# Residuals preset in PSUM by ScalarE for all but two tiles, and the copies of the down weights in other places, in an attention and FP4 feed-forward kernel

## The chip, the cores and the metric

The kernel runs on one core of a Trainium2 chip. The metric is the device time of one execution in microseconds. The engines are TensorE (PE, with its weight loads as PEld), VectorE (DVE), ScalarE (ACT), GpSimd (POOL) and the queue that SyncE issues (SPq).

## The reference

The input `x` is 64 sequences of 128 rows of 256. What is computed, cut to what matters here:

```
x  = x + xattn(layernorm(x), ctx, ctx, Wq, bq, Wout, bout)   # correlation, top 12 shifts, weighted rolls
xn = layernorm(x)
gate = q(xn) @ q(w_gate).T ;  y = q(xn) @ q(w_up).T           # 256 -> 704
h = silu(gate) * y
out = x + q(h) @ q(w_down).T                                  # 704 -> 256
```

`q` is a blockwise quantization to FP4 and back: each block of 16 values is divided by its largest magnitude / 6, set on a grid of 8 magnitudes with a sign, and multiplied by that scale again. The last line holds what the change is about: the product with the down weights and the addition of `x`, the residual.

## The kernel before

The first part (to about 90 us of the span) loads `x` and the context, does the attention, quantizes the weights and turns most of them. The feed-forward part then goes over 64 tiles of 128 rows, in 32 pairs (NP = 32). Every engine has its own list of work, written out by hand, in stages of one pair; semaphores with constant counts tie the lists together. There is no planner.

In stage n **TensorE** (the loop at L1130) does `down` of tile 2n-7, `gate_and_up` of tiles 2n and 2n+1, and `down` of tile 2n-6. `gate_and_up` (L1108) fills three PSUM banks per tile: 18 products, six of 512 columns for each of two banks and six of 384 for the third. Behind the second bank ScalarE may start SiLU (`silu`, L711), behind the third VectorE may multiply (`gate_up`, L1375). `down` (L1066) is 17 products of 256 columns into one bank, 6 or 7 in turn for most tiles.

The residual can be added in two ways. For a **preset** tile, TensorE first opens the bank with one product of 256 columns (`open_down`, L1128, ahead of the third bank of a `gate_and_up`); it has to wait until the result of the tile two before, which stands in the same bank, has been read (`out_ready`, L293). ScalarE then overwrites the bank with the scaled tile of `x` (`preset_x`, L782), `down` accumulates onto it, and ScalarE writes the scaled sum to SBUF (`residual` of ScalarE, L716). For an **added** tile there is no opening and no presetting: `down` starts a new sum, and VectorE scales it and adds `x` in one instruction (`residual` of VectorE, L1457). Before, the added tiles are 1, 5, 9 ... 53, fourteen in all; tiles 0 to 61 without these are preset, 48 in all; the last two have an addition of their own on VectorE (L1451).

**ScalarE** in stage st (the loop of `for st in range(1, END)`) does, in this order: result of tile 2st-8 (L716), squares of a later pair (L753), the scales (L764), result of tile 2st-7, SiLU of tile 2st, preset of tile 2st-6, normalising of pair st+3 (L743), SiLU of tile 2st+1, preset of tile 2st-5, then the split of h of pair st-1 (`split_h`, three long instructions of 1408 columns, L650, L651, L653) and the split of x of pair st+2 (`split_x`, the same three lines with 512 columns).

**VectorE** in stage st does the two products of pair st-1 (L1375), their block maxima (L1492), the grid steps of pair st-2 (`offset_h`, which waits for ScalarE's split of h, L1172; `grid_h`, `high_h`) and of x, the added residual if there is one, the inverse scales (L1511), the products of x, and the scaling of h (L1486) and x (L1479). **GpSimd** does the low halves of h (L545) and adds the attention result to `x` (L599). **SyncE** issues the transposing transfers of h and x, the stores and the loads of the attention result, in order.

The **down weights** are turned on TensorE in five fills, numbers 8 to 12 (`transpose_weights`, L978), into banks 6 and 7, and copied to SBUF by ScalarE (`evacuate_weights`, L338 and L339). Fills 8 and 9 are turned ahead of the loop. Before, fill 10 is turned behind pair 0, fill 11 inside pair 2, fill 12 behind pair 2. ScalarE copies fill 8 ahead of its loop, fill 9 in stage 1 behind the first SiLU, fill 10 at the end of stage 1, fill 11 in stage 2 behind the first SiLU, fill 12 in stage 2 behind the second SiLU and ahead of the split of h. `filler` puts products without use on TensorE where it would have to wait.

Of the kernel before, what the change touches and what calls it, by code (L numbers as in the profile page):

```python
# [87 lines left out]
def build(nc, x, ctx, wq, bq, wout, bout, w_gate, w_up, w_down, out):  # L88
    es = ExitStack()
    with es:  # L90
# [182 lines left out]
        def tile_ok(i):  # L273
            return 0 <= i < B

        def added(i):
            return i % 4 == 1 and i // 2 < NP - 4

        def preset(i):
            return not added(i) and 0 <= i < 2 * NP - 2  # L280

        def n_added(i):
            return (min(i, 2 * (NP - 4) - 1) + 3) // 4

        def n_preset(i):
            return i + 1 - n_added(i)
# [355 lines left out]
        def _(act):  # L642
# [141 lines left out]
            def residuals(i):  # L784
                if tile_ok(i) and not added(i):
                    residual(i)
# [50 lines left out]
            for st in range(1, END):  # L837
                j, n = st - 1, st + 2
                if st < NP:
                    residuals(2 * st - 8)  # L840
                    square_x(st + 4)
                    scale_high(st)
                    residuals(2 * st - 7)
                    silu(2 * st)
                    preset_x(2 * st - 6)
                    if st <= 2:
                        evacuate_weights(act, range(GU_FILLS + 2 * st - 1, GU_FILLS + 2 * st))
                    normalise_x(st + 3)
                    if st == NP - 1:
                        split_h(j)  # L850
                        preset_x(2 * st - 5)
                    silu(2 * st + 1)
                    if st == 2:
                        evacuate_weights(act, range(GU_FILLS + 4, len(FILLS)))
                    if st < NP - 1:
                        preset_x(2 * st - 5)
                        split_h(j)
                    split_x(n)
                    if st == 1:
                        evacuate_weights(act, range(GU_FILLS + 2, GU_FILLS + 3))  # L860
                elif st == NP:
                    residual(2 * NP - 8)
                    preset_x(2 * NP - 6)
                    preset_x(2 * NP - 5)
                    last_split(0)
                    residual(2 * NP - 7)
                    preset_x(2 * NP - 4)
                    preset_x(2 * NP - 3)
                    residual(2 * NP - 6)
                    residual(2 * NP - 5)  # L870
                    last_split(1)
                    residual(2 * NP - 4)
                    keep_turned(0)
                    keep_turned(1)
                    residual(2 * NP - 3)
                    keep_turned(2)
                    keep_turned(4)
# [3 lines left out]
        def _(pe):  # L881
# [63 lines left out]
            def filler(n, k):  # L945
                for _ in range(n):
                    pe.matmul(bank(k)[:, 0:P], ones[:, :], ident[:, :], start=True, stop=True)  # L947
# [160 lines left out]
            def gate_and_up(i):  # L1108
                if i == 0:
                    pe.wait_ge(s["f_turned"], 16)  # L1110
                else:
                    pe.wait_ge(xT[(i // 2) % 2], 16 * (i // 4 + 1))
                need(pe, s["h_steps"], K_H * ((i - 2) // 2) + 1 + i % 2 if i >= 2 else 0)
                gu_bank(i, 0)
                gu_bank(i, 1).then_inc(s["gate_done"], 1)
                if i == 6:
                    pe.wait_ge(s["w_ev"], len(FILLS))
                if i >= 6:
                    open_down(i - 6)
                gu_bank(i, 2).then_inc(s["gu_done"], 1)  # L1120

            def open_down(j):
                if tile_ok(j) and preset(j):
                    if j // 2 == NP - 3:
                        pe.wait_ge(s["h_steps"], K_H * (NP - 1) + 1)
                    else:
                        out_ready(pe, j - (4 if j // 2 == NP - 2 else 2))
                    pe.matmul(bank(down_bank(j))[:, 0:D], ident16[:, :], dT_hi[:, 0, :], start=True, stop=False).then_inc(s["o_open"], 1)  # L1128

            for n in range(NP + 4):  # L1130
                if n == NP:
                    open_down(2 * NP - 6)
                    open_down(2 * NP - 5)
                if n == NP + 2:
                    out_ready(pe, 2 * NP - 5)
                    turn_last(0)
                if tile_ok(2 * n - 7):
                    down(2 * n - 7)
                if n == NP + 2:
                    turn_last(1)  # L1140
                if n == NP:
                    open_down(2 * NP - 4)
                if pair_ok(n):
                    if n == 2:
                        pe.wait_ge(s["w_ev"], GU_FILLS + 2)
                        filler(5, 7)
                    gate_and_up(2 * n)
                    if n == 2:
                        transpose_weights(GU_FILLS + 3)
                    gate_and_up(2 * n + 1)  # L1150
                if n == 0:
                    pe.wait_ge(s["w_ev"], GU_FILLS + 1)
                    filler(7, 6)
                    transpose_weights(GU_FILLS + 2)
                if n == 2:
                    pe.wait_ge(s["w_ev"], GU_FILLS + 3)
                    filler(12, 6)
                    transpose_weights(GU_FILLS + 4)
                if tile_ok(2 * n - 6):
                    down(2 * n - 6)  # L1160
                if n == NP:
                    open_down(2 * NP - 3)


        @block.vector
        def _(dve):
# [437 lines left out]
            for st in range(2, END):  # L1604
# [5 lines left out]
                if st < NP:  # L1610
                    if pair_ok(p):
                        offset_h(p)
                    scales(st)
                    if pair_ok(p):
                        grid_h(p)
                    if pair_ok(xa):
                        offset_x(xa)
                    if pair_ok(p) and st < NP - 1:
                        high_h(p)
                    if pair_ok(xa):  # L1620
                        grid_x(xa)
                    if tile_ok(2 * st - 7) and added(2 * st - 7):
                        residual(2 * st - 7)
                    inverses(st)
                    if pair_ok(xa):
                        products_x(xa)
                    if scaled(st):
                        dve.wait_ge(sc, 2 * (st - SC0) + 2)
                    if pair_ok(j):
                        scaling_h(j)  # L1630
                    if st == NP - 1:
                        high_h(p)
                        turned_product(p, 0, 1).then_inc(s["z_lo"], 1)
                    if pair_ok(xb):
                        scaling_x(xb)
                    largest_x(st + 3)
# [42 lines left out]
```

## Time and profile before

| | |
|---|---|
| time, median of 3 runs | 466.32 us (466.32 to 467.92) |
| the profiled execution: its time, its span | 466.81 us, 465.0 us |
| busy, share of the span: PE, DVE, ACT, POOL | 95%, 93%, 88%, 54% |
| chain that ended last: PE, ACT, DVE | 68%, 4%, 3% |
| L1128 opening products | x48 |
| L782 presets, L716 results on ACT | x48, x48 |
| L1457 added residuals on DVE | x14 |
| clock granted to TensorE, the 40 slices of the page | 9 (nine tenths or more) in each |

A share of busy time is a mean over the whole span; the attention part ahead of 90 us differs from the feed-forward part. In the rows further down, the first number of a line of the timeline is the start in the span, the second the length, and the square bracket gives how long the engine had been idle and who released it. An instruction of ScalarE or VectorE can start some 0.1 us ahead of the end of the one before it, so its price in a full list is the distance from start to start.

### The profile page before, as it was taken

Reading aid. Unit: us, or ns where it says so; the run is one execution under the profiler, and the core shown is the slowest. Engines: PE = TensorE matmul, PEld = TensorE weight load, DVE = VectorE, ACT = ScalarE, POOL = GpSimd, SP = SyncE. Lnnn points to the kernel's source line nnn. Section 1 sums busy time; section 2 is a strip of 40 time slices with the busy share of each in tenths; the row PEclk is TensorE's granted clock in tenths of the full one; section 3 lists DMA queues with packets and bytes.
Section 4 is the critical chain, followed back from the end, with each engine's and each line's share of the span. In section 5 each row is a group of like instructions: output and inputs, shape, how many; then the busy total and the mean of one; then the engine's idle time right before and its main releaser. Section 6 shows DMA issues by size and latency. Waiting matters only on the chain.

```text
span 465.0 us, 10105 instructions
## 1 busy us (share of the span) xinstructions
PE 443.0 (95%) x3436; PEld 298.7 (64%) x3436; DVE 431.3 (93%) x766; ACT 408.7 (88%) x710; POOL 252.7 (54%) x346
## 2 busy tenths in 40 slices
PE   4889998998989999999999999999999999999997
PEld 4778887755555666666666666666666666666676
DVE  3699979789899999999999999999999999999894
ACT  3369979889999999999999999999999999987684
POOL 4167772573555555666655566666666666433330
PEclk9999999999999999999999999999999999999999
DMA  7999911252446666665666766656656675656653
GB/s 241 339 348 350 357 43 35 69 137 46 90 93 141 140 141 130 149 132 131 131 132 130 137 138 143 141 130 143 142 132 134 139 143 111 128 111 132 122 122 94
DMA packets 162003, 67.95 MB, mean 146 GB/s; under 512 B 126368, under 2 KB 161696, under 8 KB 161952
## 3 DMA queue, kind: packets, MB, share of 16 engines
q1 hardware_dynamic: 161952, 67.31, 61.7%
q8 instruction: 27, 0.44, 0.4%
q14 instruction: 24, 0.20, 0.1%
HBM read 27.38 MB, written 9.18 MB: 79 GB/s over the span
## 4 chain that ended last, share of the span: by engine, by line
PE 68%; ACT 4%; DVE 3%; issue 2%; DVEq 0%; ACTq 0%
PE ps L1083 15%; PE ps L1061 14%; PE ps L1063 14%; PE ps L1062 14%; PE ps L1086 8%; PE ps L1128 2%; ACT h_c L653 1%; ACT h_c L650 1%; DVE y_h L1486 1%; PE ps L947 1%; DVE bm L1511 0%; ACT ps L782 0%; PE ps L1096 0%; ACT a_xT L716 0%; DVE ctx_sb L1380 0%
## 5 line engine op out<-in xcount | busy, mean ns | idle before, releaser
L1061 PE MATMUL ps<-guT_hi,a_xT 128*128 128x512 f16 (+1 forms) x384 | 138.7, 361 | 4.1 <-DVE hb L1375 3.0
L1063 PE MATMUL ps<-guT_hi,a_xT 128*128 128x512 f16 (+1 forms) x384 | 138.7, 361 | 0.0
L1062 PE MATMUL ps<-guT_lo,a_xT 128*128 128x512 f16 (+1 forms) x384 | 138.7, 361 | 0.0
L1083 PE MATMUL ps<-dT_hi,hqT 128*128 128x256 f16 x704 | 124.4, 273 | 0.4 <-ACT ps L782 0.3
L545 POOL TENSOR_TENSOR ctx_sb<-w_q_lo,sl 128x704 f16<-128x704 f16 x60 | 90.2, 1523 | 4.1 <-DVE ctx_sb L1443 4.1
L1086 PE MATMUL ps<-dT_lo,hqT 128*128 128x256 f16 x384 | 87.3, 273 | 0.0
L1083 PEld LDWEIGHTS ps<-dT_hi,hqT 128*128 128x128 f16 x704 | 68.9, 98 | 10.4 <-ACT ps L782 0.7
L599 POOL TENSOR_TENSOR xs<-xs,w_raw 128x512 f32<-128x512 f32 x30 | 38.4, 1279 | 64.2 <-DVE ctx_sb L1380 57.8
L561 POOL TENSOR_TENSOR sl<-bm,sh 128x240 f16<-128x240 f32 (+2 forms) x33 | 31.1, 941 | 74.9 <-DVE y_h L1486 72.0
L711 ACT ACTIVATE w_raw<-ps,inv_gu 128x704 f32<-128x704 f32 x64 | 53.8, 840 | 15.8 <-PE ps L1063 15.6
L1061 PEld LDWEIGHTS ps<-guT_hi,a_xT 128*128 128x128 f16 x384 | 37.6, 98 | 38.6 <-issue 2.7
L1063 PEld LDWEIGHTS ps<-guT_hi,a_xT 128*128 128x128 f16 x384 | 37.6, 98 | 38.5
L1062 PEld LDWEIGHTS ps<-guT_lo,a_xT 128*128 128x128 f16 x384 | 37.6, 98 | 32.0
L1375 DVE SCALAR_TENSOR_TENSOR hb<-ps,h_in,w_raw 128x704 f32<-128x704 f32 x64 | 57.6, 936 | 0.1
L650 ACT ACTIVATE h_c<-y_h 128x1408 bf16<-128x1408 bf16 (+3 forms) x39 | 47.8, 1225 | 8.7 <-DVE y_h L1190 4.5
L1492 DVE TENSOR_REDUCE bm<-hb 128x88 f32<-128x1408 f32 x31 | 50.2, 1620 | 1.1
L653 ACT ACTIVATE h_c<-h_c,root 128x1408 bf16<-128x1408 bf16 (+3 forms) x39 | 50.8, 1303 | 0.0
L1486 DVE TENSOR_TENSOR y_h<-hb,bm 128x1408 f32<-128x1408 f32 x31 | 50.0, 1612 | 0.1
L651 ACT ACTIVATE h_t<-y_h 128x1408 f16<-128x1408 bf16 (+3 forms) x39 | 47.2, 1211 | 0.0
L1086 PEld LDWEIGHTS ps<-dT_lo,hqT 128*128 128x128 f16 x384 | 37.6, 98 | 5.8
L743 ACT ACTIVATE w_q_hi<-xs,s_nmr,s_r 128x256 f32<-128x256 f32 x62 | 33.6, 593 | 0.7 <-POOL s_nmr L593 0.7
L1172 DVE TENSOR_TENSOR h_t<-h_c,h_t 128x1408 f16<-128x1408 bf16 (+3 forms) x39 | 30.8, 791 | 3.2 <-ACT h_c L653 3.1
(189 smaller groups left out, 813.2 us busy)
## 6 DMA issues: line engine op xcount, KB each, us to landing
xs<-in_x_dram SPq DMA_DIRECT2D x16, 512.0 KB, 8.7
ctx_sb<-in_ctx_dram SPq DMA_DIRECT2D x16, 512.0 KB, 8.3
out_dram<-a_xT SPq DMA_DIRECT2D x64, 128.0 KB, 2.1
w_raw<-a_scratch SPq DMA_DIRECT2D x60, 128.5 KB, 2.7
hqT<-ctx_sb SPq DMA_TRANSPOSE x62, 3.7
w_raw<-in_L_ffn_w_down_dram SPq DMA_DIRECT2D x1, 704.0 KB, 8.1
w_raw<-in_L_ffn_w_gate_dram SPq DMA_DIRECT2D x1, 640.0 KB, 5.1
w_raw<-in_L_ffn_w_up_dram SPq DMA_DIRECT2D x1, 640.0 KB, 6.4
```

The source lines that it names most:

```text
L545: pool.tensor_tensor(hq[:, j % 2, t, FF:2 * FF].rearrange("p (ih r) -> p ih r", ih=IH), h_g.bitcast(F16).rearrange("p (ih t r) -> p t ih r ...
L650: act.activation(c.bitcast(BF16), top, ACT.Square, scale=ANCHOR_SLOPE * unit).then_inc(done, 1)
L653: act.activation(c.bitcast(BF16), c.bitcast(BF16), ACT.Square, bias=root[:, 0:1]).then_inc(done, 1)
L711: act.activation(sil[:, i % 2, :], gu_out(i)[:, 0:FF], ACT.Silu, scale=inv_gu[:, 0:1]).then_inc(s["sil_done"], 1)
L1061: pe.matmul(dst, xt[:, c, :], guT[0][:, c, n0:n1], start=(c == 0), stop=False)
L1062: pe.matmul(dst, xt[:, c, :], guT[1][:, c, n0:n1], start=False, stop=False)
L1063: last = pe.matmul(dst, xt[:, KC + c, :], guT[0][:, c, n0:n1], start=False, stop=(c == KC - 1))
L1083: last = pe.matmul(dst, hqT[:, j % 4, c, :], dT_hi[:, c, :], start=(c == 0 and not preset(j)), stop=(c == DCH - 1))
L1086: pe.matmul(dst, hqT[:, j % 4, c, :], dT_lo[:, c, :], start=False, stop=False)
L1375: dve.scalar_tensor_tensor(out=h_v, in0=gu_out(i)[:, FF:2 * FF].rearrange(split, ih=IH), scalar=h_in[:, 0:1], in1=sil[:, i % 2, :].rearran ...
L1486: dve.tensor_tensor(y_h[:, :].rearrange(runs, ih=IH, il=2), hb[:, :].rearrange(runs, ih=IH, il=2), bm[:, 2, 0:RUN_H].unsqueeze(1).unsqueez ...
L1492: dve.tensor_reduce(bm[:, 0, 0:RUN_H], hb[:, :].rearrange("p (ih b il) -> p b ih il", ih=IH, il=2), AX.XY, ALU.max, apply_absolute_value=T ...
```

## The change

The added tiles are now 0 and 1 alone, so tiles 2 to 61 are preset: 60 in place of 48. VectorE's list looks at both tiles of its stage, so it does the residuals of tiles 0 and 1 one behind the other in stage 4. The opening products begin in `gate_and_up(8)`, and the one of tile 61 is issued behind `down(59)` in place of ahead of it. On ScalarE fill 9 is copied at the end of stage 1, fills 10 and 11 at the end of stage 2, fill 12 at the start of stage 3. On TensorE fills 10 and 11 are turned behind pair 2, fill 12 between the two tiles of pair 3, with other counts of useless products; the wait for all copies goes from the inside of `gate_and_up(6)` to the place ahead of `down(0)`.

```
@@ added, n_added
-            return i % 4 == 1 and i // 2 < NP - 4
+            return i in (0, 1)
-            return (min(i, 2 * (NP - 4) - 1) + 3) // 4
+            return min(i, 1) + 1
@@ ScalarE, for st in range(1, END)
                 if st < NP:
+                    if st == 3:
+                        evacuate_weights(act, range(GU_FILLS + 4, len(FILLS)))
                     residuals(2 * st - 8)
...
                     preset_x(2 * st - 6)
-                    if st <= 2:
-                        evacuate_weights(act, range(GU_FILLS + 2 * st - 1, GU_FILLS + 2 * st))
                     normalise_x(st + 3)
...
                     silu(2 * st + 1)
-                    if st == 2:
-                        evacuate_weights(act, range(GU_FILLS + 4, len(FILLS)))
...
                     split_x(n)
                     if st == 1:
-                        evacuate_weights(act, range(GU_FILLS + 2, GU_FILLS + 3))
+                        evacuate_weights(act, range(GU_FILLS + 1, GU_FILLS + 2))
+                    if st == 2:
+                        evacuate_weights(act, range(GU_FILLS + 2, GU_FILLS + 4))
@@ TensorE, gate_and_up
-                if i == 6:
-                    pe.wait_ge(s["w_ev"], len(FILLS))
-                if i >= 6:
+                if i >= 8:
                     open_down(i - 6)
@@ TensorE, for n in range(NP + 4)
                     if n == 2:
-                        pe.wait_ge(s["w_ev"], GU_FILLS + 2)
-                        filler(5, 7)
+                        filler(5, 6)
                     gate_and_up(2 * n)
-                    if n == 2:
-                        transpose_weights(GU_FILLS + 3)
+                    if n == 3:
+                        transpose_weights(GU_FILLS + 4)
                     gate_and_up(2 * n + 1)
                 if n == 0:
                     pe.wait_ge(s["w_ev"], GU_FILLS + 1)
                     filler(7, 6)
+                if n == 2:
+                    filler(10, 6)
                     transpose_weights(GU_FILLS + 2)
-                if n == 2:
-                    pe.wait_ge(s["w_ev"], GU_FILLS + 3)
-                    filler(12, 6)
-                    transpose_weights(GU_FILLS + 4)
+                    transpose_weights(GU_FILLS + 3)
+                if n == 3:
+                    pe.wait_ge(s["w_ev"], len(FILLS))
+                if n == NP + 1:
+                    open_down(2 * NP - 3)
                 if tile_ok(2 * n - 6):
                     down(2 * n - 6)
-                if n == NP:
-                    open_down(2 * NP - 3)
@@ VectorE, for st in range(2, END)
-                    if tile_ok(2 * st - 7) and added(2 * st - 7):
-                        residual(2 * st - 7)
+                    for i in (2 * st - 8, 2 * st - 7):
+                        if tile_ok(i) and added(i):
+                            residual(i)
```

## Rows read from the trace of the kernel before

**Rows 1.** Stretch, busy us of PE, PEld, DVE, ACT, POOL; clock, DMA share, GB/s.
```profile
233.00:284.00 51.00, 51.00 (x337) 32.45 (x335) 50.83 (x70) 49.02 (x80) 32.36 (x38) 1.00 0.65 137
```

**Rows 2.** Timeline of ScalarE, stages 14 and 15 (start, length, engine, line, work).
```profile
250.78 0.46 ACT L716 ACTIVATE a_xT<-ps,inv_out 128x256 f32<-128x256 f32 x1
...
253.14 0.47 ACT L782 ACTIVATE ps<-xs,out_fac 128x256 f32<-128x256 f32 x1
253.54 1.09 ACT L743 ACTIVATE w_q_hi<-xs,s_nmr,s_r 128x256 f32<-128x256 f32 x2
255.17 0.85 ACT L711 ACTIVATE w_raw<-ps,inv_gu 128x704 f32<-128x704 f32 x1 [0.54 <-PE ps L1063]
255.92 0.47 ACT L782 ACTIVATE ps<-xs,out_fac 128x256 f32<-128x256 f32 x1
256.40 1.38 ACT L650 ACTIVATE h_c<-y_h 128x1408 bf16<-128x1408 bf16 x1
...
261.96 0.46 ACT L716 ACTIVATE a_xT<-ps,inv_out 128x256 f32<-128x256 f32 x1
...
272.99 0.45 ACT L716 ACTIVATE a_xT<-ps,inv_out 128x256 f32<-128x256 f32 x1
```

**Rows 3.** Timeline of TensorE, the opening product of tile 22, stage 14.
```profile
251.28 0.28 PE L1128 MATMUL ps<-dT_hi,ident 128*128 128x256 f16 x1
```

**Rows 4.** Timeline of TensorE, first products of tiles 56, 58 and 60.
```profile
404.14 0.38 PE L1061 MATMUL ps<-guT_hi,a_xT 128*128 128x512 f16 x1
...
415.20 0.38 PE L1061 MATMUL ps<-guT_hi,a_xT 128*128 128x512 f16 x1
...
426.18 0.38 PE L1061 MATMUL ps<-guT_hi,a_xT 128*128 128x512 f16 x1
```

**Rows 5.** Timeline of VectorE, stages 2 to 4.
```profile
115.11 0.89 DVE L1172 TENSOR_TENSOR h_t<-h_c,h_t 128x1408 f16<-128x1408 bf16 x1 [0.55 <-ACT h_c L653]
...
120.05 1.61 DVE L1486 TENSOR_TENSOR y_h<-hb,bm 128x1408 f32<-128x1408 f32 x1
...
127.55 0.89 DVE L1172 TENSOR_TENSOR h_t<-h_c,h_t 128x1408 f16<-128x1408 bf16 x1 [1.32 <-ACT h_c L653]
...
135.22 1.79 DVE L1375 SCALAR_TENSOR_TENSOR hb<-ps,h_in,w_raw 128x704 f32<-128x704 f32 x2
...
141.85 0.47 DVE L1457 SCALAR_TENSOR_TENSOR a_xT<-ps,inv_out,xs 128x256 f32<-128x256 f32 x1
```

**Rows 6.** Timeline of ScalarE: copy of fill 9, and the split of h in stage 2.
```profile
108.46 1.01 ACT L339 ACTIVATE dT_hi<-ps 128x1024 f16<-128x1024 f16 x1
...
123.52 1.37 ACT L650 ACTIVATE h_c<-y_h 128x1408 bf16<-128x1408 bf16 x1
```

**Rows 7.** Timeline of TensorE, tile 8: its first product and the opening inside it.
```profile
136.30 0.38 PE L1061 MATMUL ps<-guT_hi,a_xT 128*128 128x512 f16 x1 [0.82 <-DVE hb L1375]
...
140.21 0.28 PE L1128 MATMUL ps<-dT_hi,ident 128*128 128x256 f16 x1 [1.16 <-ACT a_xT L716]
```

**Rows 8.** Timelines of TensorE, ScalarE and VectorE near the end.
```profile
450.98 0.28 PE L1128 MATMUL ps<-dT_hi,ident 128*128 128x256 f16 x1 [0.33 <-ACT a_xT L716]
451.10 0.27 PE L1083 MATMUL ps<-dT_hi,hqT 128*128 128x256 f16 x1
...
451.71 0.46 ACT L716 ACTIVATE a_xT<-ps,inv_out 128x256 f32<-128x256 f32 x1
453.53 0.27 ACT L722 ACTIVATE sh<-bm 128x88 bf16<-128x88 f32 x1
...
455.95 0.52 DVE L1172 TENSOR_TENSOR w_q_lo<-w_q_lo 128x704 f16<-128x704 bf16 x1 [0.64 <-ACT w_q_lo L730]
```

**Rows 9.** TensorE's first work (timeline); the last microsecond, columns of rows 1.
```profile
7.34 1.06 PE L900 MATMUL ps<-ident,xs 128*128 128x128 f32 x4
...
11.54 0.60 PE L890 MATMUL ps<-ident,ctx_sb 128*128 128x128 f32 x4
...
464.00:465.00 1.00, 0.00 (x0) 0.00 (x0) 0.00 (x0) 0.00 (x0) 0.00 (x0) 0.81 0.08 27
```

## The prediction

> **What bounds the kernel now.** I read the busy times by stretch first. In the middle TensorE and VectorE are both full (51.00 and 50.83 of 51 us) and ScalarE is busy 49.02 of 51 [rows 1], so the share of busy time doesn't name one bound; the question is which ring of waits closes last. For that I took ScalarE's timeline, stage by stage, from the result of one tile 2st-8 to the next: 250.78 to 261.96 to 272.99, so 11.18 and 11.03 us, 22.21 for two stages [rows 2]. Then TensorE's timeline where ScalarE has little left to do, near the end: a stage with two openings takes 11.06 us (404.14 to 415.20), one with a single opening 10.98 (415.20 to 426.18) [rows 4]. That is what TensorE alone needs.
>
> The reader is to see a ring between ScalarE and TensorE. ScalarE writes the result of tile 2st-8 at 250.78; the opening product needs its bank and starts at 251.28, 0.04 us behind the end of that instruction [rows 2, 3]. From there TensorE runs without a pause to the second bank of the next tile, and ScalarE's SiLU waits for that at 255.17, having been idle 0.54 us. Behind SiLU come the preset, the split of h and the split of x, and then the next result at 261.96 [rows 2]. The length of this ring is 4.39 (250.78 to 255.17) + 0.75 (SiLU, to 255.92) + the preset + 5.56 (256.40 to 261.96). The preset costs 0.40 from start to start where nothing is waited for (253.14 to 253.54) and 0.48 at 255.92, where the split also waits for VectorE's scaled h [rows 2]. So the ring without VectorE is 4.39 + 0.75 + 0.40 + 5.56 = 11.10 us.
>
> **The middle.** Removed: one addition on VectorE in every second stage, twelve net (fourteen less the two new early ones), 0.47 us each or about 0.40 from start to start; 4.8 us of VectorE's work in all. Added for each: a preset (0.40) and a result (about 0.36, 0.46 long less the usual overlap) on ScalarE and an opening of 0.11 us on TensorE. In the even stages the second result goes in ahead of the first SiLU. The ring doesn't pass there: it is covered by the 0.54 us that ScalarE waits ahead of the second SiLU [rows 2], and 0.18 of that is left; without this cover each such stage would cost up to 0.36. In the odd stages the second preset comes between SiLU and the split of h, on the ring. There it meets a wait: the odd stage now takes 11.03 without a preset in that place, so 0.32 of its time is waiting for VectorE, who will be early. The odd stage goes from 11.03 to 11.10, the even one from 11.18 to 11.10 as the wait for VectorE (0.08) goes. Two stages: 22.20 against 22.21. TensorE with two openings in each stage needs 11.06 and so stays just under the ring. The 22 stages from 5 to 27 give 0.0 (from -0.2 to +0.1). VectorE gets slack that nothing uses.
>
> What it could be from both sides: if the ring did not bind, TensorE's 11.06 would, 22 x 0.045 = 1.0 us faster; if ScalarE's 0.18 were not enough, by 0.1 in each of 12 double stages, 1.2 us slower. I take the ring as it adds up.
>
> The Trainium skill, "ScalarE: Activation LUTs", in the part on the steps of an ACTIVATE, says that ScalarE writes to PSUM faster than to SBUF. By that the preset (to PSUM) would cost less than the result's 0.36, the ring would fall under TensorE's 11.06, and the middle would give up to -1.0 us. The rows have it the other way round: 0.47 long into PSUM, 0.46 into SBUF [rows 2], so I keep 0.40.
>
> **The start.** VectorE waits for ScalarE's split of h twice, 0.55 us at 115.11 and 1.32 at 127.55 [rows 5]. The copies stood ahead of these splits: fill 9 at 108.46 (1.01 us), fills 11 and 12 ahead of the split at 123.52 [rows 6]. With fill 9 behind the split, the first wait goes. The second split can then start when the scaled h of pair 1 is there, at 120.05 + 1.61 - 0.55 = 121.1 [rows 5] in place of 123.52, 2.4 earlier, and so the second wait goes as well. What is late next: VectorE itself, whose stage 4 would start at 135.22 - 0.55 - 1.32 = 133.35 [rows 5]. Fills 10 to 12 now cost ScalarE about 2.1 us (three copies of 0.5 to 0.9) between the split of x in stage 2 and the SiLUs of stage 3; queued behind them are these SiLUs and the split of h of pair 2, and VectorE waits for that. By my walk it comes only some 0.1 us ahead of need, so this cover is thin, and anything beyond it is passed on 1 to 1. TensorE turns fill 12 between the tiles of pair 3 and must wait for the copy of fill 10 there, about 0.7 us, which nothing on the ring sees.
>
> Then the gain is taken back. Tile 0 is now added by VectorE, behind the grid steps of stage 4, where tile 1 was: at 141.85 - 1.87 = 139.98, done 0.47 later at 140.45 [rows 5]. The opening of tile 2 inside tile 8 must wait for it. Before, it waited for ScalarE and stood at 140.21 [rows 7]. So TensorE, though it starts tile 8 about 1.1 us earlier (the gap ahead of 136.30 closes [rows 7]), stands at the opening for some 2.7 us and goes on at 140.4, 0.2 us later than before. Everything in the ring hangs on this place. **+0.2**, from +0.1 to +0.6.
>
> **The last stages.** Stage 27 now ends without a preset ahead of its split of h; with it the ring takes 11.10 and TensorE, which before could go on at its own pace there, opens tile 50 about 0.14 later. Tile 53 gets an opening in a stage where TensorE is the bound: 0.08 (11.06 less 10.98) to 0.11 [rows 4]. **+0.24**, from 0 to +0.3.
>
> **The end.** The opening of tile 61 stood at 450.98 and had waited, 0.33 us by the profile and about 0.5 in distance [rows 8]. Now `down(59)` goes first and starts about 0.5 earlier; 17 products at 0.11 (450.98 to 451.10 is 0.12 [rows 8]) put the opening at 450.98 - 0.5 + 1.86 = 452.34. But ScalarE's preset of tile 61 waits for it, and behind it in ScalarE's list stand the results of 58 and 59 and the scales of the last tile's split, for which VectorE waits at 455.95 [rows 8]. The result of 58 stood 0.73 behind the opening (451.71); it comes to 453.07, and two instructions of 0.36 to 0.38 later the scales start at 453.81 against 453.53. TensorE's 0.5 is lost, as it then waits for the last tiles' grid. **+0.28**, from -0.5 (if TensorE's order is all that counts) to +0.3.
>
> **The sum.** 0.0 + 0.2 + 0.24 + 0.28 = 0.7 us onto the profiled execution: span 465.0 to 465.7, its time 466.81 to 467.5. That execution is 0.5 above the median of 466.32, so the median becomes 467.0. No change from the old time can be told within 0.5% (2.3 us), and this is 0.15%.
>
> **The rivals.**
> *The clock falls in the long stall (the slower side).* TensorE's clock rose only some time after it began: four transposes take 1.06 us at 7.34 and 0.60 at 11.54. It fell again in the last microsecond (0.81 on the mean of it), in which TensorE issued nothing [rows 9]. The pause of 1.16 us at tile 8 [rows 7] left it at full clock; the new one of some 2.7 us is more than twice as long. If it falls to 1.2 GHz there, it stays so for up to 4.2 us (7.34 to 11.54), and half of these is lost, 2.1 us, with no slack in the ring to take it up: 467.0 + 2.1 = 469.1. It decides if the longer pause at tile 8 is enough for the clock to fall as it did at the end. Against it: useless products still fill stage 2, and tile 8 has work right before and behind. The Trainium skill, "TensorE: Matmul & The Clock Gate", Part 1, says just this: an array that has been idle is put back to half its clock and gets it back only after sustained work. Chance 0.25.
>
> *The start keeps its gain.* If the addition of tile 0 doesn't hold the opening, ScalarE is the next that is late. It follows VectorE's scaled h, which comes 1.87 earlier [rows 5] less 0.40 for the second addition, 1.5: 467.0 - 0.2 - 1.5 = 465.3. Against it: the order in VectorE's list is fixed, and 140.45 already assumes that both its waits are gone. Chance 0.08.
>
> *TensorE alone sets the pace.* VectorE's full 50.83 of 51 [rows 1] speaks for VectorE as the bound of today, and 4.8 us of it go. But TensorE's 11.06 caps that: -1.0, and the late 0.14 of stage 27 goes too: 465.8. For it: the ring is only 0.04 longer. Chance 0.15; with the rival before it, 464.2 or a little less, 0.05 of further chance.
>
> *ScalarE is short of room in its stage*, in steady stages or by the copies of stage 3 (beyond the 0.1 of cover): 1 to 2.5 us slower, up to 469.5. Chance 0.07.
>
> **How the numbers follow.** The forecast of 467.0 has 0.40, and by its bounds 466.0 to 467.6 for itself. The range goes from 465.0 (just below the case in which the start keeps its gain) to 469.1 (the clock falls). Faster by over 0.5% (under 464.0) takes two rivals at once, or a gain that I don't see: 0.08. Slower by over 0.5% (above 468.65) is most of the clock's chance and a part of the last: 0.24. The rest, 0.68, is no difference that can be told.
>
> **What would show it.** Right: L782 and L716 x60 and L1457 x2; two stages in the middle at 22.2 us; ScalarE's stages of 11.10 each, no longer 11.18 and 11.03; VectorE with gaps of some 0.2 us per stage; no gaps of VectorE at its 1st and 2nd `offset_h`; a pause of 2 to 3 us ahead of the first opening, released by VectorE's L1457 at about 140.4; preset of tile 61 waiting for TensorE. Wrong: stages of 11.06 or less, an opening of tile 2 ahead of 140, ScalarE's second SiLU without a wait in even stages, or a granted clock below 1 about 140 us.

## The result, and the profile after

The changed kernel takes 469.0 us in the median (466.69 to 470.09, 22 runs), the kernel before 466.62 (466.29 to 469.32, 22 runs alternating with it). The ratio is 1.0037, 95% interval 1.0025 to 1.0049: 1.7 us slower, clear of zero and inside the 0.5% that I had called no difference, while the medians lie 2.4 us apart. The profiled execution took 469.47 us, its span 467.7.

The page of the changed kernel: its busy times, the clock by slices, and the chain that ended last (each entry a share of the span).

```profile
PE 445.0 (95%) x3444; PEld 300.2 (64%) x3444; DVE 430.8 (92%) x754; ACT 415.0 (89%) x734; POOL 251.3 (54%) x346
...
PEclk9999999999998999999999999999999999999999
...
PE 69%; DVE 6%; issue 1%; ACT 0%; DVEq 0%; ACTq 0%
```

ScalarE left the chain (4% before), VectorE came up from 3% to 6%. One clock slice reads 8. That slice is a mean over 11.7 us, so short stretches follow. Their columns are those of [rows 1]; the last but two is the clock as a share of full speed.

```profile
233.00:284.00 51.00, 51.00 (x338) 32.47 (x336) 50.83 (x69) 50.04 (x86) 31.91 (x37) 1.00 0.63 133
80.00:84.00 4.00, 3.66 (x9) 2.56 (x10) 1.57 (x3) 3.12 (x5) 3.02 (x2) 0.58 0.00 0
142.00:145.00 3.00, 3.00 (x10) 1.12 (x9) 3.00 (x6) 0.98 (x2) 0.46 (x1) 0.52 0.44 106
```

The reader is to see two stretches near half speed (1.2 GHz), at 81 and at 142; I call each a fall. The kernel before shows 1.00 in both stretches in its profile (the one at 80 stands further down):

```profile
142.00:145.00 3.00, 3.00 (x18) 1.54 (x17) 3.00 (x5) 2.45 (x6) 1.47 (x2) 1.00 0.03 6
```

The timeline of TensorE at tile 8, which answers to [rows 7]:

```profile
136.03 0.38 PE L1061 MATMUL ps<-guT_hi,a_xT 128*128 128x512 f16 x1
...
138.19 0.38 PE L1062 MATMUL ps<-guT_lo,a_xT 128*128 128x512 f16 x1
138.40 0.38 PE L1063 MATMUL ps<-guT_hi,a_xT 128*128 128x512 f16 x1
141.17 0.28 PE L1126 MATMUL ps<-dT_hi,ident 128*128 128x256 f16 x1 [2.39 <-DVE a_xT L1455]
141.29 0.33 PE L1061 MATMUL ps<-guT_hi,a_xT 128*128 128x384 f16 x1
...
142.84 0.63 PE L1062 MATMUL ps<-guT_lo,a_xT 128*128 128x512 f16 x1
143.26 0.63 PE L1063 MATMUL ps<-guT_hi,a_xT 128*128 128x512 f16 x1
...
145.68 0.38 PE L1063 MATMUL ps<-guT_hi,a_xT 128*128 128x512 f16 x1
145.89 0.38 PE L1061 MATMUL ps<-guT_hi,a_xT 128*128 128x512 f16 x1
```

From the last product of the second bank to the opening 2.77 us pass (1.54 before). A microsecond later the products of 512 columns stand 0.43 apart in place of 0.21, until 145.4. The opening was released by VectorE's addition of tile 0. VectorE's timeline of the same kernel, which answers to [rows 5]:

```profile
115.32 0.88 DVE L1170 TENSOR_TENSOR h_t<-h_c,h_t 128x1408 f16<-128x1408 bf16 x1
...
126.34 0.88 DVE L1170 TENSOR_TENSOR h_t<-h_c,h_t 128x1408 f16<-128x1408 bf16 x1
...
134.01 1.79 DVE L1373 SCALAR_TENSOR_TENSOR hb<-ps,h_in,w_raw 128x704 f32<-128x704 f32 x2
...
140.64 0.87 DVE L1455 SCALAR_TENSOR_TENSOR a_xT<-ps,inv_out,xs 128x256 f32<-128x256 f32 x2
```

Both its waits for the split of h are gone. The fall at 81 had already moved everything here later: from the first of the last three fills ahead of the loop (TensorE, L990, at 77.69) to the opening pass 63.48 us, and 62.08 to 62.26 in profiles of this start without that fall. In the middle (ScalarE, answering to [rows 2]) each stage is 11.09 long, 253.24 to 264.33 to 275.41:

```profile
253.24 0.45 ACT L716 ACTIVATE a_xT<-ps,inv_out 128x256 f32<-128x256 f32 x1
...
257.63 0.85 ACT L711 ACTIVATE w_raw<-ps,inv_gu 128x704 f32<-128x704 f32 x1 [0.19 <-PE ps L1063]
258.38 0.47 ACT L782 ACTIVATE ps<-xs,out_fac 128x256 f32<-128x256 f32 x1
258.78 1.36 ACT L650 ACTIVATE h_c<-y_h 128x1408 bf16<-128x1408 bf16 x1
...
264.33 0.46 ACT L716 ACTIVATE a_xT<-ps,inv_out 128x256 f32<-128x256 f32 x1
...
275.41 0.46 ACT L716 ACTIVATE a_xT<-ps,inv_out 128x256 f32<-128x256 f32 x1
```

And the end, ScalarE and VectorE, answering to [rows 8]. The preset of tile 61 waits 1.36 for TensorE:

```profile
455.06 0.48 ACT L782 ACTIVATE ps<-xs,out_fac 128x256 f32<-128x256 f32 x1 [1.36 <-PE ps L1126]
455.47 0.82 ACT L716 ACTIVATE a_xT<-ps,inv_out 128x256 f32<-128x256 f32 x2
456.18 0.27 ACT L722 ACTIVATE sh<-bm 128x88 bf16<-128x88 f32 x1
458.62 0.53 DVE L1170 TENSOR_TENSOR w_q_lo<-w_q_lo 128x704 f16<-128x704 bf16 x1 [0.86 <-ACT w_q_lo L730]
```

Where the 2.67 us between the spans (465.02 and 467.69) arose, by the starts of four opening products (tiles 2, 4, 50, 56) in the two profiles:

| section | before | after | difference |
|---|---|---|---|
| start to the opening of tile 2 | 140.21 | 141.17 | +0.96 (the fall at 81 in it) |
| to the opening of tile 4 | 11.17 | 12.78 | +1.61 (the fall at 142 in it) |
| to the opening of tile 50 | 255.35 | 255.04 | -0.31 |
| to the opening of tile 56 | 33.10 | 33.25 | +0.15 |
| to the end of the span | 25.20 | 25.45 | +0.25 |

The runs themselves come in steps, by the mean clock of each. The second fall above lasts 3.4 us (142.1 to 145.5). That takes 0.0036 off the mean, so 0.996 is one fall and 0.993 two. The mean doesn't say where a fall lies; only a profile does. The kernel before is shown by its 77 runs beside the experiments, in three groups, as its 22 runs above have no clock on record:

| mean clock | changed: runs, median us | before, 77 runs: runs, medians of the three groups |
|---|---|---|
| 1.000, 0.999 | 3, 466.74 | 56, 466.5 to 466.8 |
| 0.996 | 10, 468.5 | 16, 467.7 to 468.1 |
| 0.993 or less | 9, 469.84 | 5, single runs of 468.5 to 470.5 |

So the question was the clock, and beneath it whether the rest of the sum held.

### The profile page after: what moved, and what is told of

The parts are those of the page before. It is cut to its first block, busy times and chain, and to the rows that moved or that the text cites. A ratio compares the mean times of both kernels' runs of the same rounds, so it can differ in the third digit from the quotient of the medians.

```text
span 467.7 us, 10133 instructions
## 1 busy us (share of the span) xinstructions
PE 445.0 (95%) x3444; PEld 300.2 (64%) x3444; DVE 430.8 (92%) x754; ACT 415.0 (89%) x734; POOL 251.3 (54%) x346
## 4 chain that ended last, share of the span: by engine, by line
PE 69%; DVE 6%; issue 1%; ACT 0%; DVEq 0%; ACTq 0%
PE ps L1083 16%; PE ps L1061 14%; PE ps L1063 14%; PE ps L1062 14%; PE ps L1086 9%; PE ps L1126 2%; DVE hb L1373 1%; DVE y_h L1484 1%; DVE bm L1490 1%; DVE bm L1514 1%; DVE w_q_lo L1427 0%; DVE ctx_sb L1378 0%; DVE x_c L1174 0%; DVE h_t L1170 0%; DVE x_t L1170 0%
```

## The experiments

Line numbers are those of each kernel. Ratios are to the kernel before.

**Useless products in the pause** (the changed kernel and this):

```
+                if i == 8:
+                    filler(10, 2)
                 if i >= 8:
                     open_down(i - 6)
```

> The changed kernel, with 20 useless products (10 calls of filler, each two passes, some 2.2 us at 0.11 each) into the free third bank of tile 8, ahead of the opening of tile 2. Theory (clock): the 2.8 us pause at tile 8 makes the granted clock fall to half there, and a fall costs 1.5 to 2.1 us; with the pause filled, no fall near 142 us is left in any run, while the opening still stands where VectorE's addition of tile 0 lets it (about 140.3, plus what an earlier fall adds). The median drops from 469.0 to 467 to 467.7, and only the earlier fall near 81 us (1.0 to 1.5 us) still spreads the runs. Rival (the pause itself or ScalarE's longer list costs the 2.4 us): no change, 469.0.

467.74 us (12 runs), ratio 1.0013 (0.9993 to 1.0033). Six runs have full clock, with a median of 467.18; five have one fall, and one, the profiled, lost three times as much. Its profile happened to have two early falls (20 and 81 to 88 us), and still:

```profile
141.51 0.38 PE L1063 MATMUL ps<-guT_hi,a_xT 128*128 128x512 f16 x1
141.73 2.39 PE L947 MATMUL ps<-ident,ones 128*128 128x128 f32 x20
144.07 0.28 PE L1128 MATMUL ps<-dT_hi,ident 128*128 128x256 f16 x1
144.19 0.33 PE L1061 MATMUL ps<-guT_hi,a_xT 128*128 128x384 f16 x1
```

Behind the opening the clock stays full, and the stage from tile 2's opening to tile 4's is 11.09 in place of 12.78. It is TensorE's idle time that brings the second fall, not the lateness of the opening: that comes almost as late behind the second bank as in the changed kernel (2.56 us against 2.77). Full-clock runs went from 3 of 22 to 6 of 12; that the falls left are all early ones is shown by one profile only. The full-clock runs are 0.4 slower than the changed kernel's, and why stays open.

**The pause taken away**: the additions of tiles 0 and 1 go ahead of the grid steps in VectorE's stage 4.

```
                 if st < NP:
+                    for i in (2 * st - 8, 2 * st - 7):
+                        if tile_ok(i) and added(i):
+                            residual(i)
                     if pair_ok(p):
                         offset_h(p)
...
-                    for i in (2 * st - 8, 2 * st - 7):
-                        if tile_ok(i) and added(i):
-                            residual(i)
```

> The changed kernel with one thing moved: VectorE adds tiles 0 and 1 at the start of its stage 4, ahead of the grid steps of h, in place of behind those of x. Theory: VectorE's late addition of tile 0 holds TensorE's opening of tile 2 and takes back the gain of the moved copies; moved, the pause at tile 8 shrinks from 2.8 us to under 1, the granted clock stays full there, and the start keeps 1.1 to 1.5 us of its gain. Then about 465.3 with the clock full all the way and 466.5 with a fall near 81 us. Rival (something else, ScalarE's result or copies, holds the opening as well): the opening of tile 2 stays at 140 or later and the time at 467 or more.

466.34 us (12 runs), 0.9984 (0.9972 to 0.9995). Five are at full clock, with a median of 465.33, which is 1.4 under the changed kernel's 466.74. Seven have one fall, with 466.51; in the profile it is the one at 81. TensorE at tile 8 of this kernel runs through:

```profile
138.48 0.38 PE L1062 MATMUL ps<-guT_lo,a_xT 128*128 128x512 f16 x1
138.69 0.38 PE L1063 MATMUL ps<-guT_hi,a_xT 128*128 128x512 f16 x1
138.91 0.27 PE L1126 MATMUL ps<-dT_hi,ident 128*128 128x256 f16 x1
```

So the moved copies had earned 1.4 us, and the place of tile 0 in VectorE's list was handing it back, with a fall of the clock on top: 19 of the changed kernel's 22 runs had at least one fall, there or at 81.

**The fall at 81.** `e9_earlyfill` is that kernel with useless products between the last transposes ahead of the loop; `e11_beforefill` is the kernel before with the same:

```
             for f in range(EARLY + 1, GU_FILLS):
                 transpose_weights(f)
+                filler(1, 5)
+            filler(2, 5)
```

> The kernel with tiles 0 and 1 added early in stage 4 (as in e2_early), and five more calls of filler (ten useless products, 0.22 us a call) in TensorE's pauses between 77 and 81 us, one behind each turned fill of the gate and up weights and two ahead of the wait for the shifted weights. Theory: these pauses (1.2, 0.4, 0.4, 0.9 us) make the clock fall near 81 us in about half the runs, at 1.2 to 1.4 us each; filled, it does not fall there, the runs no longer spread, and the median goes from 466.34 to 465.3 to 465.5. Rival (the falls have another cause, or the 1.2 us pause ahead of 78 that is left decides): still falls in half the runs, median 466.3 or more.

> The kernel before with nothing but the five calls of filler between 77 and 81 us. Theory: about a quarter of the runs of the kernel before have a fall of the clock there (467.8 in place of 466.5); filled, all stay full: median 466.3 to 466.6, hardly under its own 466.6, but no run above 467.3. That makes it the fair partner for e9_earlyfill: the moved copies with the early addition are then worth about 1.1 us by themselves. Rival: the falls of the kernel before lie elsewhere and stay.

The first: 465.39 (12 runs), 0.9958 (0.9942 to 0.9974), all twelve at 1.000 or 0.999. The second: 466.51 (11 runs), 0.9988 (0.9979 to 0.9997), all eleven too. So the useless products take away the falls of the kernel before (21 of its 77 runs above); that those lay at 81 no profile shows. TensorE's idle stretches between 77 and 81 us are 1.05, 0.18, 0.18 and 0.77 us in the changed kernel and 0.87, 0.18, 0.19 and 0.68 in the kernel before, so the fall there follows no single long pause. The stretch from 80 to 84 in three kernels, the early additions without and with the products, then in the kernel before:

```profile
80.00:84.00 4.00, 3.73 (x9) 2.63 (x10) 1.58 (x3) 3.12 (x5) 3.02 (x2) 0.57 0.00 0
```

```profile
80.00:84.00 4.00, 3.77 (x20) 2.98 (x20) 2.35 (x6) 3.80 (x7) 3.02 (x2) 1.00 0.02 7
```

```profile
80.00:84.00 4.00, 3.09 (x15) 2.36 (x14) 2.46 (x6) 3.75 (x7) 3.04 (x2) 1.00 0.05 12
```

(The third is the kernel before, in a run that kept its clock.) At half speed nine products get done in these 4 us, at full speed fifteen, and the useless ones besides. With both falls out of the way the comparison is clean: the change with its order mended is 1.1 us faster (465.39 against 466.51; spans 463.54 and 464.64), and no run of one reaches into the other's (465.70 at most against 466.36 at least).

**The middle as it was**: every fourth tile (1, 5 ... 53) added again, tile 0 left, and the count in `n_added` to match.

```
-            return i in (0, 1)
+            return i == 0 or i % 4 == 1 and i // 2 < NP - 4
```

> The changed kernel, with tiles 5, 9 ... 53 added by VectorE again (as before the change) and only tiles 0 and 1 otherwise as changed. So this is the moved copies and the addition of tile 0 alone, without the twelve more presets. Theory: the presets of the middle and the end are worth nothing that matters (the middle -0.3, the end +0.15 by the two traces), so this runs within 0.4 us of the changed kernel, 468.6 to 469.4, with the same pause and the same fall of the clock at tile 8. In the trace ScalarE's stages are 11.18 and 11.03 again. Rival (ScalarE's longer list costs the time): it returns to about 466.6.

468.58 us (12 runs), 1.0038 (1.0024 to 1.0052), against the changed kernel's 1.0037. The section between the openings of tiles 4 and 50 is 254.91 in place of 255.04. Its first stages are 10.96 and 11.08 while VectorE is ahead, and from stage 11 on 11.18 and 11.03, as before. The extra presets move the time by nothing that can be seen, as forecast; but it is VectorE that sets the old pace, on which more below.

**The tail as it was**: the opening of tile 61 back behind `down(58)`.

```
-                if n == NP + 1:
-                    open_down(2 * NP - 3)
                 if tile_ok(2 * n - 6):
                     down(2 * n - 6)
+                if n == NP:
+                    open_down(2 * NP - 3)
```

> The changed kernel with the opening of tile 61 back in its old place, ahead of down(59). Theory: in the new place ScalarE's preset of tile 61, and behind it the results of 58 and 59 and the scales of the last split, wait for TensorE; that costs 0.28 us. Put back, runs in which the clock stays full go from 466.7 to 466.4 to 466.5, those with one fall from 468.5 to 468.2. In the trace the last L722 follows the opening of tile 60 sooner and TensorE has its pause of 0.6 ahead of down(59) again. Rival (TensorE's order counts): 0.3 to 0.5 slower than the changed kernel.

468.68 us (12 runs), 1.0033 (1.0011 to 1.0054). The two full-clock runs have 466.59 (466.74 in the changed kernel), the five with one fall 468.55 (468.5). The last section took 25.63 in its profile: TensorE waited 0.6 there for transposing transfers of `hqT`, which it doesn't in the changed kernel's. Inconclusive by itself.

**The ring made shorter**: the next result of ScalarE goes ahead of the split of x, so that TensorE's opening no longer waits for 1.7 us of splitting.

```
-                    residuals(2 * st - 8)
                     square_x(st + 4)
...
+                    if st >= 4:
+                        residuals(2 * st - 6)
                     split_x(n)
...
                 elif st == NP:
-                    residual(2 * NP - 8)
```

> The changed kernel, with ScalarE writing the result of tile 2st-6 at the end of stage st ahead of the split of x, in place of behind it at the start of the next stage. Theory: the ring of opening, SiLU, splits and result (11.09 us) holds TensorE 0.03 us per stage above its own 11.06; taken out of the ring, the split of x (1.65 us) no longer delays the opening, the stages go to 11.06 and the middle gains 22 x 0.03 = 0.7 us, the whole 0.7 to 0.9 under the changed kernel. The falls of the clock stay as they are. Rival (TensorE's own length with two openings is 11.09): no change in the stages. Rival (VectorE or the preset then waits longer): slower.

468.51 us (12 runs), 1.0029 (1.0011 to 1.0046); three at full clock, 465.95. All stages are 11.06, which is what TensorE alone needs [rows 4]; the middle section is 254.38 (-0.66), and the full-clock runs are 0.8 under the changed kernel's. Its profile has the pause ahead of the opening too (2.54 us) and no fall there.

```profile
259.60 0.46 ACT L716 ACTIVATE a_xT<-ps,inv_out 128x256 f32<-128x256 f32 x1
259.95 0.62 ACT L650 ACTIVATE x_c<-w_raw 128x512 bf16<-128x512 bf16 x1
```

**The ring made longer**: a useless copy of 96 columns on ScalarE ahead of the split of x, in 22 stages.

```
+                    if 5 <= st <= 26:
+                        act.activation(junk_a[:, :], ident[:, 0:96], ACT.Copy)
                     split_x(n)
```

> The changed kernel with one useless ScalarE copy of 128x96 in each of the stages 5 to 26, behind the split of h and ahead of the split of x: on the ring of opening, SiLU, splits and result. Theory (the ring sets the pace of the middle): each copy costs its distance from start to start, about 0.16 to 0.2, so the stages go from 11.09 to 11.25 to 11.3 and the whole gets 3.5 to 4.5 us slower than the changed kernel at the same clock. Rival (TensorE alone sets it): ScalarE has room, stages stay at 11.09.

470.72 us (6 runs), 1.0086 (1.0055 to 1.0116); four at full clock, 470.62, 3.9 above the changed kernel's. The copy costs 0.17 from start to start, and each stage with it takes 11.26:

```profile
250.15 0.27 ACT L859 ACTIVATE junk_a<-ident 128x96 f32<-128x96 f32 x1
250.32 0.62 ACT L652 ACTIVATE x_c<-w_raw 128x512 bf16<-128x512 bf16 x1
```

22 x 0.17 = 3.7: what is put on the ring is passed on one to one.

This profile shows one thing more. The pause ahead of the opening of tile 2 is as long as in the changed kernel (2.77 us from product to opening), and the clock stays full behind it:

```profile
140.05 0.28 PE L1130 MATMUL ps<-dT_hi,ident 128*128 128x256 f16 x1 [2.39 <-DVE a_xT L1459]
142.00:145.00 3.00, 3.00 (x18) 1.64 (x17) 3.00 (x4) 1.06 (x2) 1.58 (x2) 1.00 0.76 64
```

**The room beside the ring**: a useless copy on ScalarE ahead of `normalise_x`, where it waits 0.19, and one of 64 columns on VectorE ahead of the inverse scales. The second kernel has a product of two operands on VectorE instead.

```
+                    if 5 <= st <= 26:
+                        act.activation(junk_a[:, 0:64], ident[:, 0:64], ACT.Copy)
                     normalise_x(st + 3)
...
+                    if 5 <= st <= 26:
+                        dve.tensor_copy(junk_v[:, 0:64], ident[:, 0:64])
                     inverses(st)
```

> The changed kernel with one useless ScalarE copy of 128x64 in each of the stages 5 to 26 ahead of the normalising, where ScalarE has 0.19 us before the second SiLU, and one useless VectorE copy of 128x64 ahead of the inverse scales. Theory: both are off the ring. The stages stay at 11.09 (up to 11.12 if the copy is longer than 0.19), and the whole is within 0.5 us of the changed kernel at the same clock, although both engines get more work. Rival (VectorE, at 50.83 of 51 us, is the bound): VectorE's copy costs its 0.1 in each stage, 2 us or more.

> As e8_off, but VectorE's useless instruction is a multiplication of two operands, 128x64 in float, in place of a copy. In e8_off the copy of 128x64 took 1.18 us, as GpSimd's addition to x ran beside it, so that run was not the small addition it was meant to be. Theory: the copy with one operand waits for GpSimd and the form with two does not; it now costs 0.1 to 0.16 us from start to start, stays within VectorE's slack of 0.19 per stage, and ScalarE's copy (0.15) within its 0.19. The stages stay at 11.09 to 11.12 and the whole is 466.6 to 467.4 with the clock full, up to 468.6 or 470 with falls, as the changed kernel. Rival (VectorE is the bound in any case, or the place is what costs): stages of 11.2 or more, 2 us or more slower.

485.75 (4 runs), 1.039 (1.035 to 1.0431), and 486.02 (4 runs), 1.0389 (1.0359 to 1.0419); stages of 11.88 and 11.91. GpSimd and VectorE in the first of them:

```profile
249.29 0.42 DVE L1178 TENSOR_TENSOR x_c<-x_c,x_t 128x512 f16<-128x512 bf16 x1
249.46 1.29 POOL L601 TENSOR_TENSOR xs<-xs,w_raw 128x512 f32<-128x512 f32 x1 [2.16 <-DVE ctx_sb L1382]
249.63 1.18 DVE L1628 COPY junk_v<-ident 128x64 f32<-128x64 f32 x1
```

and in the second:

```profile
250.59 1.30 POOL L601 TENSOR_TENSOR xs<-xs,w_raw 128x512 f32<-128x512 f32 x1 [2.16 <-DVE ctx_sb L1382]
250.76 1.21 DVE L1628 TENSOR_TENSOR junk_v<-ident 128x64 f32<-128x64 f32 x1
```

The copy of 64 columns starts 0.17 behind GpSimd's addition and ends with it, 1.2 us later. The idea after the first, that only the form with one operand is held up, fell with the second. As a test of the room beside the ring these two say little, but they point at VectorE's rows. The kernel before, one stage with an added residual and one without, then the changed kernel:

```profile
252.94 0.47 DVE L1457 SCALAR_TENSOR_TENSOR a_xT<-ps,inv_out,xs 128x256 f32<-128x256 f32 x1
253.34 0.88 DVE L1511 RECIPROCAL bm<-bm 128x120 f32<-128x120 f32 x1
254.15 0.35 DVE L1380 TENSOR_TENSOR ctx_sb<-x_c,sh 128x512 f16<-128x512 f16 x1
...
264.12 0.89 DVE L1511 RECIPROCAL bm<-bm 128x120 f32<-128x120 f32 x1
264.94 0.59 DVE L1380 TENSOR_TENSOR ctx_sb<-x_c,sh 128x512 f16<-128x512 f16 x1
```

```profile
254.82 1.29 POOL L599 TENSOR_TENSOR xs<-xs,w_raw 128x512 f32<-128x512 f32 x1 [2.16 <-DVE ctx_sb L1378]
254.99 0.89 DVE L1509 RECIPROCAL bm<-bm 128x120 f32<-128x120 f32 x1
255.81 0.59 DVE L1378 TENSOR_TENSOR ctx_sb<-x_c,sh 128x512 f16<-128x512 f16 x1
```

The small product takes 0.35 behind an added residual and 0.59 without one. GpSimd's addition runs to 256.11 in the last block, past the product's start at 255.81; behind a residual the product starts (254.15) only when GpSimd is done (its addition, begun at 252.76, takes 1.29). So the removed addition gives VectorE not 0.40 but 11.18 - 11.03 = 0.15 a stage; the rest, 0.59 - 0.35 = 0.24, goes into the product beside GpSimd. That GpSimd is the cause is read from these rows; no run moved its addition away. The Trainium skill, "SBUF — State Buffer", under "Who interferes with whom", has it that a VectorE instruction with two inputs in SBUF contends with a GpSimd instruction that reads SBUF. The rows of the two-operand forms agree: 1.21 us for 64 columns, 0.59 in place of 0.35 for the product.

**All of it together**: the early additions, the products ahead of the loop and the shorter ring, with the tail as it was (`e10_best`) and as changed (`e12_notail`).

> All together: tiles 0 and 1 added early in stage 4, the useless products between 77 and 81 us, ScalarE's result of tile 2st-6 ahead of the split of x, and the opening of tile 61 ahead of down(59) again. Theory: 465.4 (early and filled) less 0.7 for the ring, and 0 to 0.3 for the tail: 464.4 to 464.8, in all runs with the clock full. Rival (the ring gains nothing once the start is early, since transfers or VectorE then bound): 465.2 or more.

> As e10_best, but the opening of tile 61 stays behind down(59), as in the change. Theory: the change's place costs up to 0.28, so this is 464.6 to 465.0, 0.1 to 0.3 above e10_best. Rival: the place makes no difference that can be seen, since the transposing transfers of the last tiles land at times that vary by more.

463.83 (6 runs), 0.9926 (0.9911 to 0.9941), and 463.72 (5 runs), 0.9924 (0.9909 to 0.994). Both beat the two kernels of this case, by 2.8 us and more. Both are under the 464.4 that I had expected at least. The shorter ring is worth 1.6 here (465.39 to 463.83, or to 463.72 with the same tail), twice what it gave alone: in the kernel without it the stage behind tile 2's opening was 12.18 and now is 11.06 (1.1), and the middle gives 0.5. The last sections are 25.20 and 25.45, as in the kernels with that order before and after, but the times don't differ: the tail's 0.25 is seen in the rows only.

## Why the prediction was nearly right, and where not

The forecast was 467.0 for the case that the clock holds. The three runs in which it held have 466.74. It held in 3 of 22. The rival with the clock, to which I had given 0.25, forecast 469.1, the upper end of the range, and the median is 469.0. That they lie so close is in part luck: the base was lower (466.74, not 467.0), one fall cheaper (to 468.5, not 469.1), and a second fall, which I hadn't foreseen, brings nine of the 22 runs to 469.84. The median stands between the two groups.

*The step that failed is the choice between those two.* I had the pause (2.7 forecast, 2.77 found), its place, its releaser and its price (2.1 forecast; 1.69 by the stage, 1.76 by the runs), and then set "useless products still fill stage 2, and tile 8 has work right before and behind" against it. That didn't hold. The pause of 1.54 brought no fall in the profile of before. Seven profiles have the longer one, 2.54 to 2.77. Five of them show the fall (the changed kernel 2.77, the middle as it was 2.74, the tail as it was 2.68, the two with the room beside the ring 2.56 and 2.70), and two don't (the shorter ring 2.54, the longer ring 2.77). So a pause of this length brings a fall in most executions, and its length doesn't decide in which; what does stays open. The Trainium skill, "TensorE: Matmul & The Clock Gate", Part 1, has it that the clock is set by how busy the array has been recently. The filled pause, with its full clock, agrees. What I hadn't seen at all is the fall at 81. The kernel before has falls too, in 21 of its 77 runs, and the useless products ahead of the loop take them away. Some of the 2.4 us between the medians are this one. In the two kernels whose pause at tile 8 is filled or gone, 13 of 24 runs still have a fall; why that is more than 21 of 77, when nothing ahead of 81 us was touched, stays open.

*The start.* Forecast +0.2. The openings of tile 2 themselves (139.79 to 140.59 in the five profiles of the changed start with full clock to that point, 140.21 and 139.78 before) can't tell, since what runs ahead of the last fills differs by up to 0.7 between executions. From the first of the last three of those fills to the opening it is 62.08 to 62.26, against 62.03 before and 61.95 in `e11_beforefill`: +0.1 to +0.3, so the forecast holds. The reasoning held too: both waits of VectorE gone, its list then late. The gain that I said was taken back is 1.4 by `e2_early`, and I had priced it at 1.5 in the rival in which the start keeps it.

*The middle.* Forecast 0.0 in two stages (22.20 against 22.21) and 22.18 found, so -0.3 over the section, in which I also had +0.14 for stage 27. Ring, preset (0.40) and TensorE's 11.06 came out as forecast, and two experiments moved the ring both ways. What was wrong is the other half: "VectorE gets slack", gaps of 0.2 a stage and 4.8 us of work removed. In the window VectorE is as busy as before (50.83), and 11.09 less its own 11.03 leaves 0.06. That 11.03 is VectorE's own shows where nothing is added any more and VectorE is late: in `e9_earlyfill` its block maxima stand 11.03 apart for the first stages, and 11.09 once it has caught up with the ring. The old pace was VectorE's 11.18 + 11.03, not the ring's; the two sums lie within 0.03 of each other, so the forecast was right for a reason that was half wrong, which is luck. A lone addition was priced by its own length, where it had kept the product behind it clear of GpSimd.

*The end.* Forecast 0.08 to 0.11 for tile 53's stages and 0.28 for the tail; found 0.15 and 0.25. Taken from the same point, the last scales come 0.24 later (456.18 - 442.24 against 453.53 - 439.83). That the time of the whole kernel follows isn't shown: with the two orders at the end, `e10_best` and `e12_notail` have 463.83 and 463.72.

*The sum.* Without the clock's part the sections give about +0.2 (+0.2 for the start, -0.1 for the stage behind tile 2's opening, 11.07 with full clock against 11.17, then -0.3, +0.15 and +0.25), and the full-clock medians also +0.2 (466.74 against 466.5). I said +0.7. The middle with stage 27 makes up 0.45 of the difference. The forecast of 467.0 came as close as it did because it set out from 466.32, the median of three runs, where the 22 runs have 466.62.

## What to carry to other kernels

Before an order is changed, list the places where TensorE will stand idle for longer than it did, and put the price of a fall of its clock on each: two additions of 0.4 us each in a late place of VectorE's list cost 1.4 us in waiting and, in most runs, 1.7 in clock. Read the times run by run beside the clock, since they come in steps of 1 to 2 us; here a microsecond of useless products in a thin stretch was cheap insurance. An instruction taken off VectorE is worth what its whole list becomes shorter by, with GpSimd's overlap in it, not its own length.

## What the runs showed that I had not expected

- A VectorE instruction of 64 columns took 1.18 and 1.21 us beside a GpSimd addition, in both of its forms, and made each stage 0.8 us longer (11.09 to 11.88 and 11.91).
- The fall at 142 cost 1.69 us by the stage it is in. Between the groups of runs with one fall and with none lie 1.0 to 2.0 us; only in `e10_best` a run with a mean clock of 0.996 was no longer than the rest (463.82). Useless products of about 1 us ahead of the loop took the number of full-clock runs from 5 of 12 to 12 of 12.
- The same pause doesn't always bring a fall: 3 of 22 runs of the changed kernel kept their clock, and so did the profile of `e7_on`, with 2.39 us of idle time as in the changed kernel's.
- Transposing transfers near the end land later in some kernels: TensorE waited 0.6 us for them in one profile and 1.7 in another (the middle as it was), and not at all in the changed kernel's.
